# Perceiver block on one core: GpSimd adds the two key chunks of the cross attention weights before TensorE sums them

## What is computed

```python
q = _layernorm(q, q_gamma, q_beta) * SCALE
k = _layernorm(k, k_gamma, k_beta)
attn = jax.nn.softmax(jnp.einsum('bhnd,bhmd->bhnm', q, k), axis=-1)
out = jnp.einsum('bhnm,bhmd->bhnd', attn, v)
```

## Time and profile before

| what | value |
|---|---|
| median of 3 runs | 1530.54 us |
| the profiled execution | 1513.24 us, span 1511.4 us |
| TensorE busy | 1316.6 us (87%) |
| VectorE busy | 962.9 us (64%) |
| ScalarE busy | 591.8 us (39%) |
| GpSimd busy | 447.1 us (30%) |
| chain that ended last | TensorE 85%, GpSimd 4%, VectorE 4%, issue 4% |

### The profile page before, as it was taken

The page is one execution under the profiler, slowest core; times in us unless marked ns, Lnnn a source line. Parts: engine busy times, 40 slices in busy tenths (PEclk is TensorE's granted clock), DMA queues, the critical chain, the costliest instruction groups (busy, mean ns, idle before and its releaser), DMA issues.

```text
span 1511.4 us, 58428 instructions
## 1 busy us (share of the span) xinstructions
PE 1316.6 (87%) x23912; PEld 1076.9 (71%) x23913; DVE 962.9 (64%) x2206; ACT 591.8 (39%) x1170; POOL 447.1 (30%) x436
## 2 busy tenths in 40 slices
PE   4799999999999999999999999999998628999500
PEld 3688878788788787888787888788786418888400
DVE  6466676776676666766676776677664267555433
ACT  1245444444444444444444444444443200444200
POOL 1223222222223232232222222223211101555476
PEclk9899999999999999999999999999999755999855
DMA  4601000001100000001000011100000000555676
GB/s 142 191 20 31 28 28 27 27 27 33 38 28 27 27 27 27 27 27 33 28 27 27 27 30 37 30 27 27 27 10 9 12 7 11 149 157 157 137 205 185
DMA packets 67128, 80.87 MB, mean 54 GB/s; under 512 B 8176, under 2 KB 59504, under 8 KB 66928
## 3 DMA queue, kind: packets, MB, share of 16 engines
q1 hardware_dynamic: 60016, 58.84, 12.5%
q0 software_dynamic: 6912, 18.88, 5.1%
HBM read 54.62 MB, written 23.07 MB: 51 GB/s over the span
## 4 chain that ended last, share of the span: by engine, by line
PE 85%; POOL 4%; DVE 4%; issue 4%; DMA 2%; ACT 1%; SPq 0%; POOLq 0%; DVEq 0%; ACTq 0%
PE ringB L432 15%; PE ringC L443 13%; PE oA L525 9%; PE banksS L508 8%; PE banksS L487 4%; PE banksS L727 4%; PE banksS L472 4%; POOL pt L992 3%; PE ringB L608 3%; PE ringC L432 2%; PE ringB L551 2%; PE ringB L560 2%; PE oA L432 2%; PE banksS L700 2%; PE ringB L592 2%
## 5 line engine op out<-in xcount | busy, mean ns | idle before, releaser
L804 ACT ACTIVATE pt<-banksS 128x1024 f32<-128x1024 f32 x128 | 127.7, 1024 | 121.3 <-PE banksS L508 113.2
L1116 DVE TENSOR_REDUCE mx<-banksS 128x8 f32<-128x2048 f32 x64 | 146.8, 2294 | 37.0 <-PE banksS L487 37.0
L443 PE MATMUL ringC<-wx_kv,ct 128*128 128x256 f32 x512 | 161.3, 315 | 10.2 <-POOL ct_rest L947 7.7
L443 PE MATMUL ringC<-wx_kv_rest,ct 128*128 128x256 f32 x512 | 146.6, 286 | 0.0
L443 PE MATMUL ringC<-wx_kv,ct_rest 128*128 128x256 f32 x512 | 146.0, 285 | 0.0
L508 PE MATMUL banksS<-qT,kT 17*128 17x64 f32 x4096 | 131.5, 276 | 0.9 <-DVE qT L1121 0.9
L958 POOL TENSOR_TENSOR kn<-kc,rr 128x512 f32<-128x512 f32 x64 | 68.0, 1063 | 217.2 <-DVE rr L1104 217.2
L508 PEld LDWEIGHTS banksS<-qT,kT 17*128 17x128 f32 x4096 | 122.7, 190 | 9.4 <-issue 6.4
L952 POOL TENSOR_TENSOR sc<-sc,rz 128x1024 f32<-128x1024 f32 x32 | 65.3, 2041 | 170.5 <-DVE rz L1177 170.5
L982 POOL DMA_INDIRECT pt<-normalised_rows,ids x80 | 75.8, 947 | 125.6 <-DVE ids L1341 71.0
L443 PEld LDWEIGHTS ringC<-wx_kv,ct 128*128 128x128 f32 x512 | 99.3, 194 | 16.9 <-issue 9.1
(11 more groups left out here) (220 smaller groups left out, 3028.9 us busy)
## 6 DMA issues: line engine op xcount, KB each, us to landing
ct_in<-in_ctxT SPq DMA_DIRECT2D x64, 256.0 KB, 3.1
expert_rows<-kc SPq DMA_DIRECT2D x80, 128.0 KB, 1.8
xt<-in_x SPq DMA_DIRECT2D x32, 128.0 KB, 2.1
normalised_rows<-h SPq DMA_DIRECT2D x32, 128.0 KB, 1.7
rows_without_experts<-base SPq DMA_DIRECT2D x32, 128.0 KB, 1.7
kT<-rows_without_experts SPq DMA_DIRECT2D x32, 128.0 KB, 3.0
out<-ksq SPq DMA_DIRECT2D x32, 128.0 KB, 2.6
w_down<-in_e_down SPq DMA_DIRECT2D x1, 2048.0 KB, 12.3
```

What stands on the lines that cost most here:

```text
L443: mm = pe.matmul(ringC[:, half * DIM:(half + 1) * DIM], left[:, p, k, j // 2, (j % 2) * P:(j % 2 + 1) * P], right[:, k, part * DIM:(part + ...
L804: act.activation(pt[:, g, :, :, :, :].rearrange("p i q c n -> p i (q c n)"), banksS[:, :, g * 256:(g + 1) * 256], ACT.Exp)\
L1116: dve.tensor_reduce(mx[:, 2 * r:2 * r + 2, :, HD].rearrange("p q i -> p i q"), banksS[:, :, :].rearrange("p i (q m) -> p i q m", q=2), AX. ...
```

## The change

1. `exponential` writes `pt` as before. A new GpSimd part, `weights_added`, adds the two key chunks of each quarter into a new tile `psum` (4 additions of 512 elements a tile). A new TensorE part, `weight_sums`, multiplies that sum by `head_ones`: 8 matmuls (16 instructions) a quarter in place of 16 (32). `weighted` keeps the product with the values. `heads_out` waits for both.
2. The order tables of all engines are written anew, and every lag is one lower (`LAGS` 5 to 4) but two: `load_rows` stays on 0 and `cross_biased` (GpSimd, `xres`) on 1. `load_context` was on lag 1 and is on lag 0, as is `cross_stats`: the rows `xt` are loaded in the step that uses them, and a step of the new numbering holds what a step with the next number held.
3. `at_column` (used after the dense part) takes the place of `va` in SBUF.

```diff
-LAGS = 5
+LAGS = 4
...
+        psum = sb("psum", [P, G, H // QG, 2, N])
...
             def step(s, odd):
-                on(s, odd, 5, store_rows)
-                on(s, odd, 1, load_context)
-                on(s, odd, 5, store_base)
+                on(s, odd, 4, store_rows)
+                on(s, odd, 0, load_context)
                 on(s, odd, 0, load_rows)
+                on(s, odd, 4, store_base)
...
-                for sums in range(2):
-                    at = 2 * b * P + sums * P + g * N
-                    for odd in range(2):
-                        for mc in range(2):
-                            for p4 in range(4):
-                                left = head_ones[:, odd, :] if sums else va[:, 2 * b + mc, 4 * g + p4, odd, :]
-                                mm = pe.matmul(oA[32 * p4:32 * p4 + 32, at:at + N], left, pt[:, g, 2 * (p4 % 2) + odd, p4 // 2, mc, :],
-                                               start=(odd == 0 and mc == 0), stop=(odd == 1 and mc == 1))
+                at = 2 * b * P + g * N
+                for odd in range(2):
+                    for mc in range(2):
+                        for p4 in range(4):
+                            mm = pe.matmul(oA[32 * p4:32 * p4 + 32, at:at + N], va[:, 2 * b + mc, 4 * g + p4, odd, :],
+                                           pt[:, g, 2 * (p4 % 2) + odd, p4 // 2, mc, :], start=(odd == 0 and mc == 0), stop=(odd == 1 and mc == 1))
                 mm.then_inc(ev[f"pv{q}"].sem, 1)
+
+            def weight_sums(a, p, q):
+
+                b, g = q // 2, q % 2
+                pe.wait_ge(ev[f"added{q}"].sem, ev[f"added{q}"].of(a))
+                at = 2 * b * P + P + g * N
+                for odd in range(2):
+                    for p4 in range(4):
+                        mm = pe.matmul(oA[32 * p4:32 * p4 + 32, at:at + N], head_ones[:, odd, :], psum[:, g, 2 * (p4 % 2) + odd, p4 // 2, :],
+                                       start=(odd == 0), stop=(odd == 1))
+                mm.then_inc(ev[f"zs{q}"].sem, 1)
...
+            def weights_added(a, p, q):
+                b, g = q // 2, q % 2
+                pool.wait_ge(ev[f"weights{q}"].sem, ev[f"weights{q}"].of(a))
+                if b == 0:
+                    freed(pool, ev[f"zs{2 + g}"], a)
+                else:
+                    pool.wait_ge(ev[f"zs{g}"].sem, ev[f"zs{g}"].of(a))
+                pool.tensor_tensor(psum[:, g, :, :, :].rearrange("p i q n -> p (i q) n"), pt[:, g, :, :, 0, :].rearrange("p i q n -> p (i q) n"),
+                                   pt[:, g, :, :, 1, :].rearrange("p i q n -> p (i q) n"), ALU.add).then_inc(ev[f"added{q}"].sem, 1)
...
             def step(s, odd):
-                on(s, odd, 5, ffn_rstd)
-                on(s, odd, 1, cross_rstd)
...
```

More of the change, by code:

```diff
@@ L274, in perceiver_block @@
         ev.update(chain("rz", "rz0", "rz1"))
-        for n in ("a_rstd b_rstd c_rstd k_sq0 k_sq1 k_sum0 k_sum1 kn0_ready kn1_ready pv0 pv1 pv2 pv3"
+        ev.update(chain("pv", "pv0", "pv1", "pv2", "pv3"))
+        ev.update(chain("added", *(f"added{q}" for q in range(4))))
+        ev.update(chain("zs", *(f"zs{q}" for q in range(4))))
+        for n in ("a_rstd b_rstd c_rstd k_sq0 k_sq1 k_sum0 k_sum1 kn0_ready kn1_ready"
                   " ct_ready ct_rest_ready xn_ready xres_ready q_sq q_sum qn_ready shift_ready x1n_ready x1b_ready tanh_ready mx2_ready ex_ready"
@@ L646, in step @@
             def step(s, odd):
[L647 to L678, removed]
@@ new lines, in step @@
+                on(s, odd, 3, heads_turned, "TK", 1)
+                on(s, odd, 3, heads_turned, "TQ", 0)
+                on(s, odd, 1, query_product)
+                on(s, odd, 2, maxima_turned)
+                on(s, odd, 4, ffn_rows_turned)
+                on(s, odd, 3, self_mix)
+                on(s, odd, 2, scores, 0)
+                on(s, odd, 4, route)
+                on(s, odd, 4, gate_and_up)
+                on(s, odd, 2, weighted, 0)
+                on(s, odd, 2, scores, 1)
+                on(s, odd, 2, weight_sums, 0)
@@ new lines, in step @@
+                on(s, odd, 2, weighted, 1)
+                on(s, odd, 2, weight_sums, 1)
+                on(s, odd, 1, context_product, "V0", 0, 1)
+                on(s, odd, 3, self_scores)
+                on(s, odd, 2, weighted, 2)
+                on(s, odd, 3, self_values)
+                on(s, odd, 2, weighted, 3)
+                on(s, odd, 2, weight_sums, 2)
+                on(s, odd, 4, gated_turned)
+                on(s, odd, 2, weight_sums, 3)
+                on(s, odd, 1, context_product, "V1", 1, 1)
@@ L1229, in step @@
-                on(s, odd, 1, cross_stats)
-                on(s, odd, 2, query_sums)
-                on(s, odd, 2, key_sums, 0)
-                on(s, odd, 2, key_sums, 1)
-                on(s, odd, 1, context_split)
-                on(s, odd, 2, inverse_sigmas)
-                on(s, odd, 3, heads_out, 0)
-                on(s, odd, 5, gated, 0)
-                on(s, odd, 5, routing_logits)
-                on(s, odd, 5, gated, 1)
-                on(s, odd, 4, self_maxima)
-                on(s, odd, 4, self_shifted)
@@ L1241, in step @@
-                on(s, odd, 3, heads_out, 1)
-                on(s, odd, 4, self_sums)
-                on(s, odd, 2, queries_scaled)
-                on(s, odd, 5, rows_without_experts)
-                on(s, odd, 3, cross_residual)
-                on(s, odd, 3, self_stats)
-                on(s, odd, 1, cross_normalised)
-                on(s, odd, 3, self_normalised)
-                on(s, odd, 1, keys, 0)
+                on(s, odd, 2, maxima, 0)
+                on(s, odd, 1, keys, 1)
+                on(s, odd, 4, self_residual)
@@ new lines, in step @@
+                on(s, odd, 4, ffn_stats)
+                on(s, odd, 3, self_split)
+                on(s, odd, 2, maxima, 1)
+                on(s, odd, 4, ffn_normalised)
+                on(s, odd, 1, queries)
+                on(s, odd, 2, shifted)
+                on(s, odd, 1, query_sums)
+                on(s, odd, 1, key_sums, 1)
+                on(s, odd, 0, cross_stats)
+                on(s, odd, 0, context_split)
+                on(s, odd, 4, routing_logits)
+                on(s, odd, 1, key_sums, 0)
@@ new lines, in step @@
+                on(s, odd, 1, inverse_sigmas)
+                on(s, odd, 2, heads_out, 0)
+                on(s, odd, 4, gated, 0)
+                on(s, odd, 1, queries_scaled)
+                on(s, odd, 4, gated, 1)
+                on(s, odd, 3, self_maxima)
+                on(s, odd, 3, self_shifted)
+                on(s, odd, 2, heads_out, 1)
+                on(s, odd, 3, self_sums)
+                on(s, odd, 0, cross_normalised)
+                on(s, odd, 2, cross_residual)
+                on(s, odd, 2, self_stats)
```

118 lines of the change are left out of this document (66 added, 52 removed).

## The result

| | before | after |
|---|---|---|
| median of 4 runs | 1528.8 us (1525.5 to 1530.6) | 1692.0 us (1689.8 to 1696.4) |
| profiled execution, span | 1511.4 us | 1687.7 us |
| mean step over 28 full steps | 35.32 us | 40.99 us |
| granted clock of TensorE, whole span | 0.932 | 0.874 |

The ratio is 1.107, interval 1.104 to 1.111: slower by 163 us. The forecast was 1654 (range 1512 to 1715).

The account below looks back on a forecast made before the run. TensorE, holding 85% of the chain that ended last, was taken to bound the kernel. Saving 27 us and losing 150 to waits gave +123 on 1530.5, so 1654 us; the forecast's own range 1600 to 1700, the whole 1512 to 1715.

Parts of the forecast that it names:

- the hold: VectorE's 12 small inverse_sigmas instructions wait for running GpSimd instructions, ending 12.2 instead of 5.1 us after the first scores.
- TensorE saves 27 us: TensorE's products with ones: 64 fewer instructions a tile, less one more change, saves 0.85 us a tile in 32 tiles.
- An addition takes 1.28: Each 512-element addition on GpSimd takes 1.28 us, with 1.06 as lower end and 1.5 as upper.
- The additions are hidden: In GpSimd's queue, sums needed by TensorE at 5.0 and 10.7 us are added by 4.5 and 8.7.
- One instruction in per GpSimd instruction, the rest when GpSimd is empty, end at t=12.2: VectorE's inverse_sigmas: four of 12 get in at GpSimd's changes, eight follow; t is us after a step's first scores end.
- Rival A: Small VectorE instructions are not held by GpSimd, only the saving is left: 1504 us; chance 0.20.
- B: Held VectorE instruction goes first, GpSimd's queue is some 2 us later, eating the saving: 1530 to 1542 us; chance 0.10.
- Hole of 3.9 at the transpose of `su`: TensorE's transpose of su, due at 11.2 us in the step, starts at 15.1 behind late VectorE: 3.9 lost.
- A second wait of 1.1 for the probabilities: TensorE reaches the transpose of GpSimd's self-attention probabilities at 21.1 us, they are ready at 22.2: 1.1 more lost.
- Rival C: TensorE's clock also falls behind the 3.9 us hole: +2.2 us a step, +66, 1720 us; chance 0.12.
- Sum: Waits of 5.0 us a step in 30 steps, +150, against the saving of 27: +123 us.

Follow-up runs that it names:

- e9: Changed kernel's tables and lags with the old arithmetic, no additions, and VectorE's second key_sums and inverse_sigmas ahead of cross_stats and context_split: 1531.9 us, 1.003 of before.
- e1: Changed kernel with the second key_sums and inverse_sigmas moved ahead of cross_stats and context_split in VectorE's table: 1509.5 us, 0.988 of before.
- e5: e4 with the fourth weight_sums moved behind the self attention's value product in TensorE's table: 1500.1 us, 0.983 of before.
- e4: Kernel before with its own tables and lags, only the additions and short ones-products put in: 1519.5 us, 0.996 of before.
- e8: Changed kernel with heads_out of the first half ahead of the second key_sums and inverse_sigmas in VectorE's table: 1658.6 us, 1.087 of before.
- e7: Changed kernel with each GpSimd addition replaced by a one-column addition and a memset of the rest: 1622.2 us, 1.063 of before.
- e6: Changed kernel with the self attention's score products done four times over, right ahead of the third weighted: 1674.8 us, 1.098 of before.
- e3: Changed kernel's tables and lags with the old arithmetic, no additions, ones-product over both key chunks: 1575.7 us, 1.032 of before.

## Why the prediction was right

The direction and the mechanism that starts it, the hold, were right; the place of TensorE's wait and the clock were not, and the time was 38 us short (1692 against 1654). By its steps:

- **TensorE saves 27 us: about right.** 22 us by e9 against e1, 25.6 by e5 against before. In one step of each, the products with ones take 2.18 us in e9 and 1.28 in e1, 0.9 less where 0.85 was forecast (16 instructions in 0.24 between the starts 634.48 and 634.72 of after); a longer V1 product, and a short product that waits for its addition behind the transpose of `su`, give 0.5 of it back in e1. Where the gain lies was not quite as told, see the last section.
- **An addition takes 1.28: right,** 1.288 in the mean of 128 and 1.27 where nothing else runs. The estimate of 1.12 from the Trainium skill (GPSIMD Engine Reference, § 3.1 Elementwise) is 0.15 too low for 512 elements.
- **The additions are hidden: right in GpSimd's queue.** No `weight_sums` waits for an addition in the changed kernel. In e4 the same additions in another order are not hidden.
- **One instruction in per GpSimd instruction, the rest when GpSimd is empty, end at t=12.2: right in kind,** 12.2 in the step shown, 12.5 in the mean of 27. That the number fits to 0.1 in the step shown is luck: the additions end at t=10.4, not 10.0 (the cast holds up GpSimd, last section), and two instructions slip through beside the power, so that six and not eight are left behind the last addition. Rival A falls for every GpSimd instruction of 0.7 us or more. B falls too: between these no second VectorE instruction gets in, and `ct_rest` and the additions behind it follow each other without a gap.
- **Hole of 3.9 at the transpose of `su`: the step that failed.** The prediction had `heads_out` end at t=13.4, and it did (642.99, t=13.4), but it never asked who waits for that. The third `weighted` does, at t=8.9, through a ring with one bank: 4.57 in the step shown, 4.85 in the mean. The hole of 3.9 was there behind it (e8: 3.72).
- **A second wait of 1.1 for the probabilities: did not come.** GpSimd's probabilities end at 653.15 (t=23.6), but TensorE, 3.0 later than foreseen through the earlier hole and the slow clock, comes to the transpose at 653.67 only.
- **Rival C, the clock, came true** in the size the rival had (+2.2 a step; 1.9 measured), though not at the place. It was given 0.12, on the ground that dense work follows the hole. Dense work follows, and is slow for some 4 us all the same. So the forecast's term for the clock, nothing, is the second that failed.
- **Sum.** 4.85+1.9-0.75=6.0 a step, against 5.67 measured, where the forecast had 3.9+1.1-0.85=4.15. What e1 gives back at V1 and at `su`, after doesn't: from the transpose of `su` to the end of the step it takes 22.8 in the mean, e1 23.35. The hole was 1.0 too small and the clock's 1.9 were left out, while a wait of 1.1 was counted that did not come; that the time still lies in the forecast's own range of 1600 to 1700 is partly due to this, and to the width of the range.

## What to carry to other kernels

Before work goes to GpSimd, look at which VectorE chain of short, dependent instructions with two SBUF inputs (or `TENSOR_SCALAR`) will run beside it. Here such a chain advanced by one instruction per GpSimd instruction of 0.7 us or more. Price it so, and order the tables so that the chain runs while GpSimd is empty (e1: 182 us for two moved rows). When a chain comes late, go through every handover behind it, the banks that it frees among them, and add the slow clock behind a hole like this one (1.9 us a step behind 4.85).

## What the runs showed that I had not expected

**A read and a write hold differently** (e7): an addition holds any of the twelve that starts beside it, a memset only the three `TENSOR_SCALAR`.

**The hold goes the other way too.** In the rows of after the second addition takes 1.74 instead of 1.27; it starts at 632.97, 0.08 behind VectorE's cast (632.89 to 633.58). That is no exception: in the dense part of after, up to 1250 us, 31 of GpSimd's instructions start during the cast (17 powers, 8 `x1b`, 6 additions), and each takes 0.34 to 0.53 longer than it does otherwise. The prediction's GpSimd queue had no such term.

**More work, less time** (e6): 4.2 us of repeated products in a hole of 4.6 us made the step 1.1 us shorter.

**The saving is partly in stalls.** Steps of before differ: from 527.19 to 561.80 one takes 34.61, no more than a step of e1 (34.57), while the mean is 35.32. In many of the others there are places like this one in TensorE's timeline of before:

```profile
525.49 0.44 PE L525 MATMUL oA<-pt,head_ones 128*32 128x64 f32 x17
526.83 0.43 PE L525 MATMUL oA<-pt,head_ones 128*32 128x64 f32 x15 [0.90 <-issue]
```

TensorE stops in the middle of a row of ones-instructions and waits for nothing that the profile shows. Waits of this kind from 150 to 1100 us, in before and then in e1:

```profile
PE oA L525 <- issue: 10.4, 17, 1.3
PE ringB L432 <- issue: 1.1, 1, 1.1
```

```profile
PE oA L538 <- issue: 0.2, 1, 0.2
```

11.5 us in 27 steps, 0.4 a step, shrink to 0.9 in e1 (0.7 of it at two other lines); its mean step is 0.66 shorter. What makes TensorE stop there stays open. The number of its instructions alone doesn't decide it: e9 and e3 have as many as before, and 3.3 and 1.4 us of such waits in the same stretch. e6, with 204 instructions more in a step, has 19.1.
